# Fused attention on one core: weighted sums with 128 stationary columns, row maxima in two halves, another order on SyncE

## What is computed

```python
h = concatenate([ssm(...), txt], axis=1)                 # 32 x 205 x 1024
h = h + attn(layernorm(h), wq, wk, wv, wo)
h = h + ffn(layernorm(h), W_base, b_base, enc, coefs, mask)
# attn: q, k, v = x @ wq, x @ wk, x @ wv ; causal softmax(q k^T / sqrt(32)) v ; @ wo
```

## Time and profile before

| | us |
|---|---|
| median of three runs | 3353.59 |
| the profiled execution's own time | 3349.05 |
| its span in the profile | 3347.3 |
| attention, from about 357 to 2066 us | 1709 |
| TensorE busy over the span | 3030.5 (91%) |
| VectorE busy | 2001.2 (60%) |
| ScalarE busy | 1111.7 (33%) |
| GpSimd busy | 1025.4 (31%) |

### The profile page before, as it was taken

One profiled execution on the slowest core, in us unless ns is written; L12 is line 12 of the kernel. 1 busy time (PEld: TensorE's weight loads), 2 busy tenths in 40 slices (PEclk: granted clock), 3 DMA queues, 4 the chain that ended last, 5 costly groups with the idle time before them and its releaser, 6 DMA issues. The chain is left out here.

```text
span 3347.3 us, 82139 instructions
## 1 busy us (share of the span) xinstructions
PE 3030.5 (91%) x29056; PEld 2239.5 (67%) x29056; DVE 2001.2 (60%) x4714; ACT 1111.7 (33%) x2452; POOL 1025.4 (31%) x1400
## 2 busy tenths in 40 slices
PE   1848799999999999999999997799999999999999
PEld 1637688888898888888888984244545454544444
DVE  7975576767676767676776765444444444443443
ACT  4331345454455455454545454210101010100100
POOL 3730344444444444444444454011101110110110
PEclk9978899999999999999999995599999999999999
DMA  4643222222222222222222213111221122122111
GB/s 147 169 126 106 47 79 56 80 53 80 56 80 55 79 68 65 70 63 78 55 78 56 71 48 136 38 67 59 75 75 64 68 75 75 56 75 75 69 62 46
DMA packets 235388, 249.64 MB, mean 75 GB/s; under 512 B 169753, under 2 KB 196505, under 8 KB 234785
## 3 DMA queue, kind: packets, MB, share of 16 engines
q1 hardware_dynamic: 234768, 234.69, 23.7%
q10 hardware_dynamic: 240, 10.09, 0.9%
HBM read 114.26 MB, written 80.61 MB: 58 GB/s over the span
## 5 line engine op out<-in xcount | busy, mean ns | idle before, releaser
L732 POOL TENSOR_SCALAR_AFFINE_SELECT p<-p 128x256 f32<-128x256 f32 (+1 forms) x768 | 335.3, 437 | 921.4 <-ACT p L760 899.5
L842 DVE TENSOR_REDUCE mx<-psS 77x2 f32<-77x410 f32 (+1 forms) x768 | 449.3, 613 | 242.5 <-PE psS L944 155.5
L962 PE MATMUL psJ<-xth,qh 128*128 128x205 f16 x2048 | 529.5, 259 | 10.6 <-DVE qsl L850 8.0
L964 PE MATMUL psJ<-xth,ql 128*128 128x205 f16 x2048 | 525.4, 257 | 0.0
L963 PE MATMUL psJ<-xtl,qh 128*128 128x205 f16 x2048 | 523.9, 256 | 0.0
L760 ACT ACTIVATE p<-psT,escale 128x410 f32<-128x410 f32 (+1 forms) x768 | 411.3, 572 | 282.0 <-PE psT L906 206.3
L738 POOL TENSOR_TENSOR pl<-p,ph 128x410 f16<-128x410 f32 (+1 forms) x512 | 447.1, 893 | 105.2 <-ACT ph L767 97.3
L1295 POOL TENSOR_TENSOR hb<-h,bias_sb 128x1024 f32<-128x1024 f32 x52 | 122.1, 2349 | 1045.3 <-DVE h L1337 1045.3
L929 PE MATMUL psO<-vh,pl 128*128 128x33 f16 (+2 forms) x3072 | 347.4, 187 | 0.0
L929 PE MATMUL psO<-vh,ph 128*128 128x33 f16 (+2 forms) x3072 | 341.6, 188 | 5.1 <-POOL pl L738 3.7
L929 PE MATMUL psO<-vl,ph 128*128 128x33 f16 (+2 forms) x3072 | 343.8, 187 | 0.0
(11 more groups left out here) (241 smaller groups left out, 6080.8 us busy)
## 6 DMA issues: line engine op xcount, KB each, us to landing
a_in<-acat SPq DMA_DIRECT2D x52, 512.0 KB, 4.8
h_in<-hcat SPq DMA_DIRECT2D x52, 512.0 KB, 4.2
qst<-qsh SPq DMA_DIRECT2D x512, 51.2 KB, 2.1
out<-y SPq DMA_DIRECT2D x51, 512.0 KB, 3.0
hcat<-ob SPq DMA_DIRECT2D x64, 256.0 KB, 3.7
xin<-hcat SPq DMA_DIRECT2D x32, 512.0 KB
acat<-ao SPq DMA_DIRECT2D x32, 512.0 KB
qst<-qsl SPq DMA_DIRECT2D x256, 51.2 KB, 2.1
```

Source lines behind the costliest of these rows:

```text
L732: pool.affine_select(out=v, in_=v, compare_op=ALU.is_ge, fill=0.0, base=0, pattern=[[0, v.shape[1]], [1, w]], channel_multiplier=-1).then_ ...
L842: dve.tensor_reduce(dst, v, AX.X, ALU.max).then_inc(s_read, 1)
L962: pe.matmul(ps[:, 0:S], wh[:, k, c], xth[:, par, k, :], start=k == 0, stop=False)
L964: m = pe.matmul(ps[:, 0:S], wl[:, k, c], xth[:, par, k, :], start=False, stop=k == KC - 1)
```

## The change

Three things change, all in attention.

The stationary side of every matmul of weigh() has 128 columns: h01 and h11 are read 128 columns wide, over the columns that lie behind them, and all 128 rows of the result are written; rows 77 to 127 of the second part hold values that nobody reads. So that these columns are defined, ph and pl are cleared once before the stage.

Each slot takes the maxima of one group. The transposes of the maxima are two units: m0 (the first 16 query heads of batch b + 1) in slot 4, and m1 (the other 16, of batch b) in slot 0 of the next step. Each is split and sent on its own (shift_rows), with a semaphore for each half; the scores of head 0 wait for the first half and those of head 4 for the second.

SyncE's order becomes: late queries, V, late keys, late maxima (m1), load, store, early queries, early maxima (m0), early keys.

```diff
-        mh, ml = sb("mh", [NH, S], F16), sb("ml", [NH, S], F16)
+        mh, ml = sb("mh", [NH // 2, 2, S], F16), sb("ml", [NH // 2, 2, S], F16)
...
-        m_in, v_in = sem("m_in"), sem("v_in")
+        m_in, v_in = [sem("m_in0"), sem("m_in1")], sem("v_in")
...
-        MAXES = [[0], [1], [2], [3], [4, 5], [6, 7], [], []]
+        MAXES = [[j] for j in range(NKV)]
...
+                if s == 0 and has["att"]:
+                    row.append(("m", 1))
                 if s >= 4 and has["ln"]:
                     row.append(("x", s - 4))
-                if s == NKV - 2 and has["max"]:
+                if s == 4 and has["max"]:
                     row.append(("m", 0))
...
                     wait(sp, pj_lo, before(b - 1, nxt) + at(units(prev), "q", NKV - 1) + 1)
-                    restack(K_PARTS, kst[nxt], slice(1, 2), k_in[1])
                     restack(Q_PARTS, qst[nxt], HALVES[1], q_in[1])
-                if has["load"]:
-
-                    wait(sp, pj_filled, base)
-                    pass_on(sp, passed)
-                    load(b + 4, par)
-                if has["max"]:
 
                     wait(sp, av_done, 8 * b)
                     pass_on(sp, passed)
                     sp.dma_start(vh[nxt][:], vsh[:]).then_inc(v_in, 16)
                     sp.dma_start(vl[nxt][:], vsl[:]).then_inc(v_in, 16)
+                    restack(K_PARTS, kst[nxt], slice(1, 2), k_in[1])
+                if has["att"]:
+
+                    wait(sp, pj_lo, base + at(rows, "m", 1) + 1)
+                    shift_rows(1, par)
+                if has["load"]:
+
+                    wait(sp, pj_filled, base)
+                    pass_on(sp, passed)
+                    load(b + 4, par)
...
                     restack(Q_PARTS, qst[par], HALVES[0], q_in[0])
+                if has["max"]:
+
+                    wait(sp, pj_lo, base + at(rows, "m", 0) + 1)
+                    shift_rows(0, nxt)
+                if has["qkv"]:
+
                     wait(sp, pj_lo, base + at(rows, "k", 0) + 1)
                     restack(K_PARTS, kst[par], slice(0, 1), k_in[0])
-                if has["max"]:
-
-                    wait(sp, pj_lo, base + at(rows, "m") + 1)
-                    sp.dma_start(qst[nxt][STACK:STACK + 1, :, :], mh[:]).then_inc(m_in, 16)
-                    sp.dma_start(qst[nxt][STACK + 1:STACK + 2, :, :], ml[:]).then_inc(m_in, 16)
+
+            def shift_rows(half, to):
+                heads = slice(half * (NH // 2), (half + 1) * (NH // 2))
+                sp.dma_start(qst[to][STACK:STACK + 1, heads, :], mh[:, half, :]).then_inc(m_in[half], 16)
+                sp.dma_start(qst[to][STACK + 1:STACK + 2, heads, :], ml[:, half, :]).then_inc(m_in[half], 16)
...
+            chain(pool.memset(ph[:], 0.0))
+            chain(pool.memset(pl[:], 0.0))
             pool.memset(p32[:, :, 2, :], 0.0).then_inc(const_ok, 1)
...
+                    if j == NKV // 2 and k == 0 and late_read:
+
+                        dve.wait_ge(pj_filled, base + late_read)
...
-                if g == 0 and k == 0:
+                if g % 4 == 0 and k == 0:
 
-                    pe.wait_ge(m_in, 32 * (b + 1))
+                    pe.wait_ge(m_in[g // 4], 32 * (b + 1))
...
                     def blocks(t):
-                        v = view(t, g % 2, r // 2)[:, r % 2, :]
-                        return v[:, 0:P], v[:, P:S], view(t, g % 2, 2)[:, r, :]
+
+
+                        whole = t[:, g % 2].rearrange("p k x -> p (k x)")
+                        head, tail = r * S, 2 * 2 * S + r * TXT
+                        return whole[:, head:head + P], whole[:, head + P:head + 2 * P], whole[0:TXT, tail:tail + P]
...
-                            m = pe.matmul(o[0:T[t], t, r, :], p, v[0:T[j], j, g, :],
+                            m = pe.matmul(o[:, t, r, :], p, v[0:T[j], j, g, :],
...
-                    pe.wait_ge(s_read, 24 * (b + 2))
-                    pe.transpose(ps[0:NH, 0:P], mx[:, 0, :], ident[:])
-                    m = pe.transpose(ps[0:NH, P:S], mx[0:TXT, 1, :], ident[0:TXT, 0:TXT])
+                    heads = slice(n * (NH // 2), (n + 1) * (NH // 2))
+                    pe.wait_ge(s_read, 24 * (b + 1) + 12 * (1 - n))
+                    pe.transpose(ps[0:NH // 2, 0:P], mx[:, 0, heads], ident[:])
+                    m = pe.transpose(ps[0:NH // 2, P:S], mx[0:TXT, 1, heads], ident[0:TXT, 0:TXT])
```

More of the change, by code:

```diff
@@ L608, in unit_views @@
             if kind == "m":
-                return ps[0:NH, 0:S], mh[:], ml[:]
+                return ps[0:NH // 2, 0:S], mh[:, n, :], ml[:, n, :]
             t, half = divmod(n, 2)
@@ L623, in free_place @@
             if kind == "m":
-                wait(eng, m_in, 32 * (b + 1))
+                wait(eng, m_in[n], 32 * (b + 1 - n))
         block = ctx.enter_context(nc.Block())
@@ L650, in step @@
                     wait(sp, pj_lo, before(b - 1, nxt) + at(units(prev), "q", NKV - 1) + 1)
+                    restack(Q_PARTS, qst[nxt], HALVES[1], q_in[1])
+                    wait(sp, av_done, 8 * b)
+                    pass_on(sp, passed)
+                    sp.dma_start(vh[nxt][:], vsh[:]).then_inc(v_in, 16)
+                    sp.dma_start(vl[nxt][:], vsl[:]).then_inc(v_in, 16)
                     restack(K_PARTS, kst[nxt], slice(1, 2), k_in[1])
-                    restack(Q_PARTS, qst[nxt], HALVES[1], q_in[1])
+                if has["att"]:
+                    wait(sp, pj_lo, base + at(rows, "m", 1) + 1)
+                    shift_rows(1, par)
                 if has["load"]:
@@ L657, in step @@
                     load(b + 4, par)
-                if has["max"]:
-                    wait(sp, av_done, 8 * b)
-                    pass_on(sp, passed)
-                    sp.dma_start(vh[nxt][:], vsh[:]).then_inc(v_in, 16)
-                    sp.dma_start(vl[nxt][:], vsl[:]).then_inc(v_in, 16)
                 if early and b == -1:
@@ L828, in layer_norm, with take_maxes @@
                     dve.sem_inc(dve_ln, 2)
-            def take_maxes(b, j, base, ks):
+            def take_maxes(b, j, base, ks, late_read):
                 for k in ks:
@@ L856, in step @@
                 late = None
+                late_read = at(rows, "m", 1) + 1 if has["att"] else 0
                 for g in SLOTS:
@@ L859, in step @@
                     for j in groups[:1]:
-                        take_maxes(b, j, base, (0, 1))
+                        take_maxes(b, j, base, (0, 1), late_read)
                     if late:
@@ L864, in step @@
                     for j in groups[:1]:
-                        take_maxes(b, j, base, (2,))
+                        take_maxes(b, j, base, (2,), late_read)
                     if has["att"]:
```

## The result

The kernel after took 3376.40 us in the median of four runs (3371.79 to 3380.38), against 3350.65 us (3346.96 to 3353.92) for the kernel before in the same hours: a ratio of 1.0076, 95% interval 1.0060 to 1.0092. It is some 26 us slower. I had forecast 3262, 89 us faster, and given slower a chance of 5%.

The account below looks back on a forecast made before the run. TensorE's work in attention was taken to set the time. Terms summed to -2.73 us a step, -82 over steps 0 to 29, with the start's 7.5 a total of -89: median 3262 us, range 3246 to 3280, with rivals 3240 to 3303.

Parts of the forecast that it names:

- the one on SyncE's order: SyncE's transfers in attention: V goes out earlier, its wait goes, 0.47 us a step; late keys land in time.
- Slots 2 and 3 with the wait for V: Attention slots 2 and 3: -0.31 us for the two from shorter blocks, and -0.47 from V's wait going entirely.
- Slot 7: Last slot of an attention step: gains one group of maxima, has a shorter block, +0.62 us.
- Slot 0: First slot of a step: m1 waits for q0's low part, +0.48 us, +0.1 after a jump, mean +0.29.
- the early keys: Early keys move behind two more issues, needed at 20.6 + 0.3 us; nothing charged, 0 to 1 us a step in range.
- TensorE waits for kst at a step's start: A sign named beforehand that the prediction is wrong: TensorE waiting for the keys' buffer as a step starts.
- Wide weights: Weighted sums: 24 of 36 matmuls come down by about 12.7 ns to 26 ns, 0.305 us a block, 2.44 a step.
- Rival 1: Weighted sums: a 128-column load over 77 rows goes by columns, 63 ns; 3370 us, slower than before; 5%.
- The start: Start of attention: first maxima now stand before 12 early-key issues, 7.5 us gone, first scores near 349 us.
- 2 (3303): VectorE's chain sets slots 5 to 7: 1.4 us a step, 41 us, 3303 us; 17%.
- 3 (3320): Gain in the pace only: moved waits come back elsewhere, early keys land late at each step, 3320 us; 4%.
- 4 (3232): Waits charged in slots 0, 3 and 4 vanish because VectorE is relieved: -1 us a step, 3232 us; 6%.

Follow-up runs that it names:

- e1: The kernel after with two source buffers for the projected keys (ksh, ksl), one for each parity of the step: 3272.35 us.
- e7: The kernel before with the wide weights and SyncE's late order keys, V, queries, load; maxima as before: 3269.01 us.
- e3: The kernel before with only the wide weights and the two memsets that clear ph and pl: 3295.39 us.
- e4: The kernel before with only SyncE's new order of the late transfers (late queries, V, late keys, load): 3463.65 us.
- e2: The kernel after with SyncE's late order changed to late keys, V, late queries: 3276.84 us.
- e5: The kernel after with the narrow stationary side of before (77 columns where there were 77): 3462.69 us.
- e6: e2 with the early keys sent ahead of the early queries and the first maxima: 3265.03 us.
- e8: The kernel before with only the maxima spread over the slots and split in halves; narrow weights, late keys still first: 3342.11 us.
- e10: e9 with the layer norm moved on VectorE behind the slot's normalisation of scores and the unit's low part: 3262.02 us.
- e9: e6 with the transposes of the maxima moved, m1 from slot 0 to 1 and m0 from slot 4 to 3: 3263.55 us.
- e11: e9 with the transfers of the output stage's weights moved from step -1 to step 30: 3248.20 us.
- e12: e11 with the transfers of the output stage's weights in step 31 instead of step 30: 3241.03 us.

## Why the prediction was wrong, step by step

**The step that failed** is the one on SyncE's order: "The late keys land some 19 us into the step, needed at 28." The landing is right (the last group is issued 18.4 us into step 7), and it is the wrong question. I priced where the keys arrive (the rows of scores in slot 4) and not where they leave. Their source ksh is overwritten by unit k1, which ScalarE copies in slot 1; in step 7 it was ready for that at 764.85, 11.7 us into the step, and waited 7.99 us. For V I had made just this argument, source and all. The copies of the queries don't suffer, since q4, the first to overwrite the late queries' place, is not due before slot 4. It costs 2.83 us a step in slot 2 (9.92 - 7.09), partly stall and partly the low clock behind it, which is 85 us over 30 steps, and 104 us in all, as e1 measures; of the rest, slots 0 and 7 are 0.30 and 0.19 us a step shorter in e1 too.

**With that step mended the working holds in the main.** e1 came to 3272.35, 75 us under before, where the forecast was 89; its step fell by 2.27 us, where the sum said 2.73. By slots (forecast; e1 against before):

- Slot 1: -0.31; -0.31. Slots 2 and 3 with the wait for V: -0.78; -0.31 - 0.47 = -0.78. The wait for V went entirely, as forecast.
- Slots 4, 5, 6: -0.09, -1.57, -0.89; -0.22, -1.55, -0.88.
- Slot 7: +0.62; +0.75. The jump grew. Idle at the first scores for no semaphore, in the kernel after (us in total, times, longest):

```profile
PE psT L920 <- issue: 46.5, 12, 4.8
```

That is 3.9 us a pass; the same row of before has 37.8 us in 12 times, 3.2 a pass. The same view gives 41 us in e7 and e3, 37 in e4, and 45 to 47 in e2, e5, e6, e8, e10; but 41 in e1, e9, e11, e12, so it goes neither with the split of the maxima nor with the weights alone. Its cause stays open.

- Slot 0: +0.29; +0.72. The wait of m1 is 0.41 us in step 7 where I had 0.6, and the slot 7.42 where I had 7.44.

```profile
760.26 0.28 PE L998 MATMUL psJ<-ident,mx 128*16 128x128 f32 x1 [0.41 <-DVE qsl L866]
```

What is missing is the early keys, which I said "just fit". Step 8 of the kernel after, whose slot 4 starts at 844.32, and then TensorE in step 9 (from 864.81):

```profile
844.97 6.38 SPq L637 DMA_DIRECT2D qst<-qsh  x8
...
855.35 2.43 SPq L637 DMA_DIRECT2D kst<-ksh  x4
857.83 3.38 SPq L637 DMA_DIRECT2D kst<-ksl  x4
861.24 2.49 SPq L637 DMA_DIRECT2D kst<-ksh  x4
```

```profile
866.74 0.39 PE L964 MATMUL psS<-kst,qst 96*128 96x128 f16 x4 [1.54 <-DMA kst<-ksh]
```

They arrive 22.4 us after slot 4's start; I had 20.4 and a need at 20.9. One group of four took 3.38 us to issue, not 2.47, and the landing after the last issue was 3 us instead of the median 1.8. I had 0 to 1 us a step for it in the range; e6 shows 0.41. "TensorE waits for kst at a step's start" was one of my own signs of being wrong, and it came: 28.4 us in 12 places, though it is the smaller of the two faults.

**Wide weights.** 25 ns for all 36, forecast 26, 25 as the lower bound: right. Rival 1 (5%) is wrong. The page "TensorE: Matmul & The Clock Gate" of the Trainium skill makes a load last by its columns in "LDWEIGHTS (loading the stationary operand)"; e5 against after shows the opposite sign here (+86 us for fewer columns). Its condition for the faster path in "Weight-path perf modes", exactly 128 weights not of FP32, fits all forms seen: 97 ns for 128 f16 columns with 128 and with 77 rows, against 124 ns for 77 columns and 143 to 146 ns for 128 of f32.

**The start.** First scores forecast at 349, measured:

```profile
352.32 0.86 PE L920 MATMUL psT<-qst,kst 98*128 98x410 f16 x2 [8.85 <-DMA qst<-ml]
```

The wait is 8.85 us instead of the 15.86 of the earlier trace rows, 7.0 of the 7.5 us forecast (12 issues of 0.62 us are 7.4; the prediction has 7.5 here and 7.6 for V). But TensorE's work before it ended 2.6 us later (343.47 against 340.88), and the start moved only from 356.74 to 352.32. Its first transpose already starts 1.2 us later (259.31 against 258.07), behind VectorE's layer norm and not behind the memsets.

**Rivals.** 2 (3303) had VectorE in slots 5 to 7: not seen, those slots are at 4.96 and 4.79. 3 (3320) had part of it right (early keys). 4 (3232) is not seen: m1 still waits 0.41 us in slot 0, and slot 4 takes 5.95 us where I had 6.09. The side on which it ended had only rival 1, at 5%: I had no rival in which a moved transfer holds the engine that rewrites its source, though the change swaps exactly such transfers. This was the error in the chances.

## What to carry to other kernels

A transfer has two ends. When the order of a queue changes, list for each transfer who waits for the data and who waits for its source to be free, with the time of each, and move none past the earlier of the two; issue in the order in which sources are rewritten (e2), or double the source (e1). A stall in the engine that sets the pace can cost more than its length, through the clock behind it: in the odd steps of the kernel after, stalls of 3.05 us in the mean lengthen their slot by 4.5, in e5 stalls of 4.12 by 7.9. And a part whose waits can move (the maxima: no gain of e1's step over e7's; e9 and e10) is better priced by the work of the engine that is waited for, not by the wait.

## What the runs showed of the hardware

The low clock behind short stalls was in the trace of before as well, and so was its price: in the earlier trace rows slot 0 behind a jump has a clock of 0.80 and takes 8.60 us, 1.64 more than the same slot at 1.00. I used it for the jump only.

A clock that differs without any edit shows in the stage that prepares the output weights. These are the windows from the last score matmul of attention to the first matmul of the output stage in the kernel before and in e3, whose edit lies in attention alone, and then in e12:

```profile
2057.30:2161.60 104.30, 68.05 (x202) 27.02 (x202) 57.01 (x72) 28.40 (x37) 5.07 (x12) 0.58 0.28 103
```

```profile
2022.20:2108.50 86.30, 47.80 (x201) 18.19 (x202) 55.94 (x72) 28.48 (x37) 5.63 (x13) 0.74 0.34 125
```

```profile
1948.10:2036.90 88.80, 46.42 (x202) 17.94 (x201) 56.39 (x74) 28.99 (x38) 6.16 (x13) 0.73 0.44 139
```

The same instructions of TensorE take 86 to 89 us at a mean granted clock of 0.73 to 0.74, and 104 to 106 us at 0.56 to 0.58 in the profiles of the other twelve kernels. Run times of one program spread by as much: of e12's six runs two were at 3223 and 3224 and four at 3239 to 3246, of e3's four three at 3288 to 3295 and one at 3314, and the kernel before beside e12 had 3320 and 3340 with five of 3349 to 3355. No kernel has two profiles here, so that this stage is what spreads is likely but not shown. But a profile of 18 us less need not be the edit's: e12's profile is 27 us shorter than e11's, of which 9 are attention's (last score matmul at 1948.60 against 1957.50) and the rest is this stage; the median gain is 7.

The time of an issue on SyncE is not one number: four took 2.43 to 3.38 us in step 8 above, and the one issue of mk in e9 11.12 us, as much as eighteen of the small ones. Such outliers decide where something "just fits"; the 15 issues of the weights, moved out of the way of two that TensorE waited for, brought 22 us at the start of the stage at once.
